# Adjacency tiles 7 to 9 issued ahead of two broadcast loads, and tile 10 cast one turn earlier, in a graph attention and convolution kernel

## The reference

```python
x = _layernorm(x + _L0_gnn_ref(x, adj, rel_pair_index, Wq, bq, Wk, bk), axis=-1)
x = _layernorm(x + _L1_gnn_ref(x, adj, weight, bias), axis=-1)
```

## Time and profile before

| | us |
|---|---|
| median of 3 runs | 165.84 |
| lowest and highest | 165.1 and 166.38 |
| the profiled execution | 166.42 |
| its span, first to last instruction | 164.7 |
| TensorE's mean granted clock | 0.994 |

### The profile page before, as it was taken

The page is one execution under the profiler, slowest core; times in us unless marked ns, Lnnn a source line. Parts: engine busy times, 40 slices in busy tenths (PEclk is TensorE's granted clock), DMA queues, the critical chain, the costliest instruction groups (busy, mean ns, idle before and its releaser), DMA issues.

```text
span 164.7 us, 2902 instructions
## 1 busy us (share of the span) xinstructions
PE 153.4 (93%) x1024; PEld 79.9 (49%) x1025; DVE 126.9 (77%) x391; ACT 74.0 (45%) x125; POOL 70.5 (43%) x83
## 2 busy tenths in 40 slices
PE   3989999999999999999979999999999999999950
PEld 3934445455454445444434486444665444444530
DVE  2997889994899999999557988798991568666681
ACT  5687459845864412874191044153112104333451
POOL 7588777777777777787604434000020000000000
PEclk9999999999999999999999999999999999999997
DMA  4999889999259999651002730000001992312233
GB/s 124 388 379 343 318 230 336 379 408 364 81 143 358 320 345 380 221 119 39 0 0 49 186 143 6 0 0 0 0 0 24 337 299 106 131 69 71 88 127 127
DMA packets 16232, 28.99 MB, mean 176 GB/s; under 512 B 4769, under 2 KB 5953, under 8 KB 16086
## 3 DMA queue, kind: packets, MB, share of 16 engines
q1 hardware_dynamic: 10742, 24.14, 42.1%
q10 hardware_dynamic: 3280, 3.07, 5.5%
q0 software_dynamic: 2192, 1.57, 4.1%
HBM read 19.83 MB, written 8.58 MB: 173 GB/s over the span
## 4 chain that ended last, share of the span: by engine, by line
PE 38%; POOL 34%; issue 11%; DVE 9%; DMA 3%; ACT 1%; POOLq 0%; DVEq 0%
POOL ed_adj L647 29%; PE acc L1374 15%; PE acc L1464 13%; POOL found L655 5%; PE tr L1464 3%; DMA found<-in_adj,top_i 2%; PE tr L1416 2%; DMA ed_i<-in_pairs 1%; PE acc L1489 1%; DVE st L895 1%; DVE y L831 1%; PE acc L1378 1%; PE tr L1453 1%; ACT y L807 0%; PE tr L1429 0%
## 5 line engine op out<-in xcount | busy, mean ns | idle before, releaser
L647 POOL DMA_INDIRECT ed_adj<-in_adj,ed_idx x47 | 48.5, 1033 | 15.8 <-issue 14.0
L1374 PE MATMUL acc<-adjT,x1s 128*128 128x512 f16 (+1 forms) x240 | 49.3, 354 | 0.0
L1306 PE MATMUL acc<-xs,adjT 128*128 128x512 f16 (+1 forms) x176 | 40.6, 379 | 0.5 <-DVE xs L868 0.5
L1374 PEld LDWEIGHTS acc<-adjT,x1s 128*128 128x128 f16 x240 | 22.8, 98 | 21.1 <-issue 0.2
L1306 PEld LDWEIGHTS acc<-xs,adjT 128*128 128x128 f16 (+1 forms) x176 | 16.3, 98 | 20.0 <-DVE xs L868 2.0
L1464 PE MATMUL acc<-whl,xs 128*128 128x512 f16 (+1 forms) x108 | 23.8, 370 | 0.0
L1464 PEld LDWEIGHTS acc<-whl,xs 128*128 128x128 f16 x108 | 10.5, 98 | 11.8
L1306 PE MATMUL tr<-xs,adjT 128*128 128x512 f16 (+1 forms) x66 | 15.2, 379 | 0.0
L698 ACT CAST adjT<-stage 128x1408 f16<-128x1408 f32 x9 | 12.3, 1362 | 6.0 <-DMA stage<-in_adj_T 5.8
L751 ACT ACTIVATE xs<-acc 128x512 f16<-128x512 f32 (+1 forms) x12 | 6.2, 538 | 11.2 <-PE acc L1378 11.2
L686 POOL DMA_INDIRECT x_dram<-wraw,back_i x1 | 1.3, 1337 | 21.5 <-DVE wraw L1224 21.5
(11 more groups left out here) (283 smaller groups left out, 230.7 us busy)
## 6 DMA issues: line engine op xcount, KB each, us to landing
stage<-in_adj_T SPq DMA_DIRECT2D x9, 704.0 KB, 7.3
x_dram<-x_sb SPq DMA_DIRECT2D x10, 256.0 KB
x_sb<-in_x SPq DMA_DIRECT2D x3, 768.0 KB, 7.2
sums_dram<-y ACTq DMA_DIRECT2D x6, 256.0 KB, 6.7
sums_dram<-xd ACTq DMA_DIRECT2D x5, 256.0 KB, 7.1
x_sb<-x_dram SPq DMA_DIRECT2D x1, 1280.0 KB, 12.2
out<-y SPq DMA_DIRECT2D x5, 256.0 KB, 2.0
stage<-in_adj_T SPq DMA_DIRECT2D x3, 384.0 KB, 5.6
```

The lines of the kernel that those rows point to most:

```text
L647: nc.gpsimd.indirect_dma_start(out=ed_adj[0:EP, c:c + 1], out_offset=None, in_=adj_flat, in_offset=bass.IndirectOffsetOnAxis(ap=ed_idx[0:E ...
L1306: last = mm(sum_bank(i)[:, :], adjT[0:width[k], k, i * P:(i + 1) * P], xs[0:width[k], half, k, :], start=(k == 0 and half == 0), stop=(k = ...
L1374: mm(mix_bank(u)[:, 0:j - i], x1s[:, half, k, f * P:(f + 1) * P], adjT[:, k, i:j], start=(k == 0 and half == 0), stop=False)
```

## The change

`CASTS_AFTER` moves the cast of tile 10 from ScalarE's turn 5 to its turn 4, right behind that of tile 9. In SyncE's queue the loads of tiles 7 and 8 move ahead of the wait for `row_stored` and the spread of `hot`; the load of tile 9 moves ahead of the wait for `col_stored` and the spread of `cols`. Tile 10 stays behind `cols`. The guards inside `load_adj` stay, and no transfer is added or taken away.

```diff
-CASTS_AFTER = {0: (4,), 1: (5,), 2: (6,), 3: (7, 8), 4: (9,), 5: (10,)}
+CASTS_AFTER = {0: (4,), 1: (5,), 2: (6,), 3: (7, 8), 4: (9, 10)}
@@
             load_adj(5)
             load_adj(6)
+            load_adj(7)
+            load_adj(8)
             sp.wait_ge(row_stored, 16)
             sp.dma_start(hot[:, :], row_dram.partition_broadcast(P)).then_inc(row_spread, 16)
-            load_adj(7)
+            load_adj(9)
             sp.wait_ge(col_stored, 16)
             sp.dma_start(cols[:, :], col_dram.partition_broadcast(P)).then_inc(col_spread, 16)
-            for t in range(8, T):
-                load_adj(t)
+            load_adj(10)
```

## The result

The changed kernel is slower: 166.38 us median against 165.13 for the kernel before (10 runs each), a ratio of 1.008 with a 95% interval of 1.0051 to 1.0109. The forecast was 165.8 and no change; the move is 0.8%, inside the 1% that the forecast counted as no change, but it is real, since the interval excludes 1. Medians and ranges here are of all runs; the ratios leave out runs more than 1.5% above the fastest of their kernel, a slower state that shows up whatever the kernel. The profiled execution took 166.55 us with a span of 164.8, where the one of before took 166.42 with 164.7. So the two traces differ by 0.1 us while the medians differ by 1.25. That is itself the first thing to explain.

The account below looks back on a forecast made before the run. GpSimd's lookups and TensorE's products behind them, meeting at the wait for `flag`, were taken to bound the kernel. All terms summed to 0: span 164.7 unchanged, 165.8 us against the median, range 165.0 to 166.8.

Parts of the forecast that it names:

- The guards: SyncE's queue: tiles 7 and 8 wait for the casts of tiles 4 and 5, so issue stays 25.1 and 27.9.
- tile 8: Before ScalarE's cast: it lands at 34.5, the 2.74 us stall is saved, worth 0 at the end.
- `hot`: Spread behind tile 8: issued near 28.3, lands at 38.4, 2.1 us before `hot_part` 0 reads it; price 0.
- the trade of stalls: VectorE waiting for ScalarE's roots: 2.3 us at row 4 traded for about 2 us at row 5.
- the bold sentence: VectorE's waits: one stall, 2.3 us at row 4, is traded for one of about 2 us at row 5.
- L: Time tile 10's load lands: 43.6 us with 1 us of queue gaps, range 42.6 to 44.7, far bound 46.1.
- The cushion: TensorE's wait for `flag` up to 84.33: losses from 20 to 83 us cost nothing up to 1.16 us.
- the prediction's own rule: At TensorE's look: VectorE resumes row 5 at L + 3.0 against 46.76; lateness less 0.35 slack plus 0.2 is waited.
- the sign of this: The profiled execution, 166.42 us, stands 0.58 over the median; used to forecast 165.8 against the median.
- Rival (b): ScalarE's turn 4, line 697: tile 10 landing from about 45.3 makes it slower, 166.6 at L = 46.1; chance 0.12.
- Rival (c): VectorE and `top_ready` get ahead: faster, but only a shorter lookup is left, -0.3 us to 165.5; chance 0.08.
- The range for it: GpSimd's lookups beside the three `hot_part`s: none to three longer by 0.32, -0.3 to +0.6 us, taken as 0.

Follow-up runs that it names:

- e4: The whole change run again, no edit, against the kernel before: 166.60 us median, ratio 1.0045 (1.0013 to 1.0077).
- e15: The whole change with all 47 lookups, run once more against the kernel before: 166.36 us median, ratio 1.0031 (0.9998 to 1.0063).
- e14: The whole change but with tile 10 issued ahead of cols, all 47 lookups, against the kernel before: 165.07 us median, ratio 0.9969 (0.9941 to 0.9997).
- e3: Only the loads moved, tile 10 still cast in turn 5, against the kernel before: 166.29 us median, ratio 1.0025; its profiled execution took 168.89 us.
- e2: Only the cast of tile 10 moved behind that of tile 9, loads in the old order, against the kernel before: 165.75 us median, ratio 0.9983.
- e12: Only the loads moved, tile 10 cast in turn 5, all 47 lookups, against the kernel before: 165.49 us median, ratio 1.0005 (0.9974 to 1.0036).
- e5: The kernel before with 44 of its 47 lookups, against the kernel before: 165.30 us median, ratio 1.0016 (0.9987 to 1.0045).
- e9: Only the loads moved, with 44 lookups, against the kernel before with all lookups: 165.25 us median, ratio 0.9999 (0.9971 to 1.0028).

## Why the prediction was wrong, point by point

**The guards, tile 8, `hot`, the trade of stalls: right.** The stall of 2.74 us at tile 8 went, `hot_part` 0 wasn't held up (41.46 us, `hot` issued at 29.47 and landed 9.2 us later), and VectorE's stall moved from row 4 to row 5, as the bold sentence said. Tile 9, behind `hot` now, made ScalarE wait 2.44 us before its cast, a stall that the prediction had not named. Nothing hangs on it, since tile 10 landed after tile 9's cast had ended.

**Tile 10's landing: the term was too small.** The prediction took L = 43.6, with 1 us of gaps in the queue and 44.7 as its own far end. The runs gave 44.7 (e4), 45.4 (the profile after) and 45.4 (e15). In the two with 45.4 some 0.7 us isn't the change's: x was split later (VectorE's last pair of splits at 17.88 and 17.73 us, against 16.88 in e4), and with it ScalarE's cast of tile 7 came at 35.12 and 34.97, against 34.10. Part of the rest are gaps in the queue. Stretches of 1 us, kernel after (the last two columns are the DMA share and GB/s):

```profile
28.00:29.00 1.00, 1.00 (x6) 0.49 (x5) 0.93 (x5) 1.00 (x2) 0.69 (x2) 1.00 0.31 45
29.00:30.00 1.00, 1.00 (x7) 0.42 (x5) 0.97 (x3) 0.97 (x3) 0.69 (x2) 1.00 0.63 231
...
43.00:44.00 1.00, 1.00 (x6) 0.46 (x5) 0.93 (x6) 0.12 (x1) 0.69 (x2) 1.00 0.75 267
```

Ahead of tile 8's issue there was little to carry, and it is paid back at 43 to 44 us, where the queue was idle before. The gaps alone don't give the delay, though: added up over stretches of 1 us from 21 us to the landing, the idle share is 1.9 us before, 2.8 in e4 and 3.0 in the kernel after, so about the 1 us that the prediction allowed, while tile 10 took 8.9 to 9.2 us from issue to landing instead of 6.6. What the rest is stays open. What the runs do show is that the place of `cols` decides: with the same loads moved and `cols` behind tile 10 (e14), tile 10's cast starts by 42.94, at most 6.9 us after its issue at 36.0. The mistake about L was small, though: at L = 45.4 the prediction's own rule gives VectorE 1.6 us late and the look a wait of 1.6 - 0.35 + 0.2 = 1.5 us, and 1.19 was measured.

**The cushion: this is the step that failed.** "The reader is to see from this that TensorE's work from 20 to 83 us has a cushion behind it ... whatever it loses there, up to 1.16 us, costs nothing." The cushion was read from one execution of 166.42 us, and it was set against runs that went down to 165.1. In the kernel before, GpSimd's string ends at 69.9 in every one of three profiles, and those executions took 166.3 to 166.7. The many near 164.8 can't contain such a string: in these three, TensorE's first matmul on `flag` comes 14.3 us or more after the string's end, and in 16 of the 17 profiles (all but e3's) the span ends 80.2 to 80.4 us after that matmul. With 1.7 us around the span, that makes 166.2 or more. e2, e12, e14 and e15, which have the same 47 lookups, end it at 67.0 to 67.8. With that end there is at most 0.2 us behind TensorE (e2), and its wait of 1.2 us goes to the end. The prediction even wrote down the sign of this, the profile 0.58 over the median, and used it only to shift the sum. Against the median of ten runs it was 1.3 over.

**The sizes of the rivals.** Rival (b) had the right mechanism, place and sign, at 0.12. Its threshold, L above 45.3, was worked out with the cushion in it. Without it the threshold is about 43.9 (VectorE late by no more than the slack of 0.15 us at the look). All three landings measured for the change are above that. (The working has two slips of 0.1 us that change nothing: 42.6 and gaps of 2 us make 44.6, not 44.7, and tile 10's issue is 35.2 in one place and 35.3 in another.) Rival (c) had said that VectorE's lead starts nothing at `top_ready`; where the string is short VectorE does set the start of the 8 lookups (1.11 us in e12), but TensorE's own work ends no earlier for it, and e12 stays at 1.0005.

**GpSimd's string.** The range for it, -0.3 to +0.6 us from the `hot_part`s, was the wrong place to look. The string varies by 2 to 3 us, and that starts before 9 us, where nothing was changed.

## What to carry to other kernels

A slack read from one profiled execution is a slack of that execution: when its time lies above the lowest ones, ask first which path was long in it, and price an edit by the other path too. A wait that is put ahead of a root or a scale costs by what stands behind it on the engine; the same late transfer cost nothing that could be measured one turn later (e12), and with the load issued one place earlier the wait was gone (e14). When a load is moved up past a broadcast, follow the last load of the queue: the bytes are the same, but the broadcast is carried later, and what stands behind it lands later.

## What the runs showed of the hardware

The difference in GpSimd's string begins in the first 5 us. (That it is the whole difference between short and long executions is not shown; see e5.) In the six profiles whose string begins at 7.3 us, VectorE reaches line 831 at 4.35 to 4.37, just after GpSimd's `iota` of 1408 columns has begun, and takes 1.26 us; in the eleven others it gets there at 4.09 to 4.14, before it, and takes 0.24 or 0.25. Timelines of GpSimd and VectorE, kernel before:

```profile
4.23 1.30 POOL L643 IOTA col_no<- 128x1408 f16 x1
4.37 1.26 DVE L831 TENSOR_SCALAR y<-ed 128x158 f32<-128x158 f32 x1
```

and e14:

```profile
4.11 0.24 DVE L832 TENSOR_SCALAR y<-ed 128x158 f32<-128x158 f32 x1
4.27 1.30 POOL L644 IOTA col_no<- 128x1408 f16 x1
```

What goes with it in all 17 profiles is when the pair list has landed. In the six, the first conversion (line 828) starts at 3.16 to 3.25, beside GpSimd's `iota` at line 634 (from 3.20), and ends at 3.63 or 3.64 whatever its start; in the eleven it starts at 3.01 to 3.13 and takes 0.24 to 0.32, and there the `iota` is the longer one, 0.27 to 0.32 us instead of 0.23 or 0.24. The index for the lookups is ready 1.27 us later in the first case. The second step is the third lookup, which takes 4.01 us in five of the six profiles, while VectorE makes six `split_x` in a row from 9.57. It takes 2.20 in the sixth, the kernel after, and in nine of the eleven, where they come in threes with a pause. Kernel before and e14:

```profile
9.57 3.68 DVE L868 SCALAR_TENSOR_TENSOR xs<-x_sb,xs 128x512 f16<-128x512 f32 x6
10.07 4.01 POOL L647 DMA_INDIRECT ed_adj<-in_adj,ed_idx  x1 [0.31 <-issue]
```

```profile
8.29 1.87 DVE L869 SCALAR_TENSOR_TENSOR xs<-x_sb,xs 128x512 f16<-128x512 f32 x3
8.79 2.20 POOL L648 DMA_INDIRECT ed_adj<-in_adj,ed_idx  x1 [0.30 <-issue]
```

In both pairs of rows the lookup ends 0.8 us after VectorE's run does. The Trainium skill, "SBUF — State Buffer", on the shared port pair, says that GpSimd and VectorE exclude each other for a whole instruction when VectorE is in a two-port mode, or has two SBUF inputs while GpSimd reads SBUF, and that the one that starts first wins. The rows on lines 643 and 831 agree with it where GpSimd starts first, and those on lines 634 and 828 in both orders. The third lookup agrees as far as the waiting goes (`split_x` has two SBUF inputs), but it waited through a whole run of instructions and not for one. That it is this lock was not tested by itself. In e9 the lookup had started first, at 8.82 against 8.98, and took 0.95 us, as the rule has it. But most of the other lookups run beside VectorE at 0.95 us, too, and in e5, without a long third lookup at all, the same three `split_x` ran beside a lookup of 1.01 us, which I can't explain.
